# Six deep attention layers: exponential per 64-key piece with q's inverse norm as its scale, four new orders of work, and the feed-forward front moved by a third of a group

## The reference, cut to what matters

```python
qkv = x @ Wqkv
q = l2norm(q) * qs                      # per token and head
k = l2norm(k) * ksc
q = q * cos * scale + rotate_half(q) * sin * scale
k = k * cos / scale + rotate_half(k) * sin / scale
sim = einsum('bhwie,bhwje->bhwij', bq, bk2) * 8.0    # 32 queries against 64 keys
sim = where(mask, -max, sim)
attn = softmax(sim, -1)
out = einsum('bhwij,bhwje->bhwie', attn, bv2)
x = x + out @ Wo
xn = (x - mu) / sqrt(var + 1e-05) * g + bln
a, gate = split(xn @ W1 + b1)
x = x + a * gelu(gate) @ W2 + b2
```

## Time and profile before

| | us |
|---|---|
| median of 3 runs | 6133.31 (6131.36 to 6148.67) |
| the profiled execution, device time | 6136.03 |
| its span, first to last instruction | 6134.2 |
| first attention layer, 1399 to 2006 | 607 |
| first feed-forward block, 2006 to 2198 | 192 |

### The profile page before, as it was taken

The page is one execution under the profiler, slowest core; times in us unless marked ns, Lnnn a source line. Parts: engine busy times, 40 slices in busy tenths (PEclk is TensorE's granted clock), DMA queues, the critical chain, the costliest instruction groups (busy, mean ns, idle before and its releaser), DMA issues. The chain is left out here.

```text
span 6134.2 us, 175865 instructions
## 1 busy us (share of the span) xinstructions
PE 4713.8 (77%) x70592; PEld 3658.9 (60%) x70592; DVE 4298.2 (70%) x6496; ACT 2838.3 (46%) x5349; POOL 3353.0 (55%) x1834
## 2 busy tenths in 40 slices
PE   4986999947887678885788866888668887678875
PEld 3664877745666456664566655666546665466664
DVE  4346999958886478873688836888358884588854
ACT  2552333315554355552455534555335554355542
POOL 0004666637775367762577725777347774367741
PEclk8897999968998789986899978999778997798887
DMA  1000000002222012220122211222102222022220
GB/s 29 0 0 19 1 0 0 0 32 57 54 54 65 4 45 54 54 62 20 38 57 56 56 28 31 54 54 54 41 18 54 54 54 55 7 52 53 54 60 22
DMA packets 151608, 229.83 MB, mean 37 GB/s; under 512 B 33038, under 2 KB 56460, under 8 KB 149900
## 3 DMA queue, kind: packets, MB, share of 16 engines
q1 hardware_dynamic: 150924, 219.36, 15.0%
HBM read 26.31 MB, written 4.19 MB: 5 GB/s over the span
## 5 line engine op out<-in xcount | busy, mean ns | idle before, releaser
L1993 POOL TENSOR_TENSOR spare<-raw,table 128x512 f32<-128x512 f32 x768 | 1318.7, 1743 | 296.5 <-ACT spare L1592 296.5
L2003 POOL TENSOR_TENSOR raw<-raw,rs 128x1024 f32<-128x1024 f32 x384 | 821.8, 2151 | 694.5 <-DVE rs L1782 694.5
L1761 DVE TENSOR_TENSOR raw<-raw,spare 128x1024 f32<-128x1024 f32 x384 | 795.8, 2072 | 13.2
L1754 DVE TENSOR_TENSOR raw<-raw,table 128x1024 f32<-128x1024 f32 x384 | 736.8, 1919 | 62.3 <-POOL spare L1993 57.8
L1400 PE MATMUL trn<-ident,E 128*128 128x128 f32 x1536 | 329.5, 353 | 475.2 <-POOL E L2031 353.7
L1804 DVE TENSOR_REDUCE mx<-sco 128x16 f32<-128x1024 f32 x192 | 235.1, 1225 | 533.9 <-PE sco L1385 533.8
L2031 POOL TENSOR_TENSOR E<-E,rden 128x1024 f32<-128x1024 f32 x192 | 447.3, 2330 | 258.2 <-DVE rden L1819 258.2
L1400 PEld LDWEIGHTS trn<-ident,E 128*128 128x128 f32 x1536 | 237.3, 182 | 550.2 <-issue 366.2
L1611 ACT ACTIVATE room<-trn 128x512 f32<-128x512 f32 x384 | 230.1, 599 | 580.5 <-PE trn L1400 580.1
L1366 PE MATMUL trn<-ident,raw 128*128 128x128 f32 x3072 | 484.7, 281 | 9.2 <-ACT kT L1600 3.8
L1748 DVE TENSOR_REDUCE ss<-spare 128x16 f32<-128x1024 f32 x384 | 464.1, 1209 | 16.5 <-ACT spare L1592 16.4
(11 more groups left out here) (220 smaller groups left out, 11388.7 us busy)
## 6 DMA issues: line engine op xcount, KB each, us to landing
Vw<-V SPq DMA_DIRECT2D x1344, 128.0 KB
Vw<-V SPq DMA_DIRECT2D x192, 64.0 KB
spare<-in_L_ffn_Wqkv SPq DMA_DIRECT2D x6, 1536.0 KB, 6.6
wo<-in_L_ffn_Wo SPq DMA_DIRECT2D x6, 512.0 KB, 3.9
X<-in_L_attn_x SPq DMA_DIRECT2D x16, 128.0 KB, 2.6
x_before_deep<-X SPq DMA_DIRECT2D x1, 2048.0 KB, 8.3
raw<-x_before_deep SPq DMA_DIRECT2D x1, 2048.0 KB, 8.0
out<-X SPq DMA_DIRECT2D x16, 128.0 KB, 2.0
```

Of the source, the lines that this page charges most:

```text
L1754: dve.tensor_tensor(x, x, table[:, part, 0, k][:, None, :].to_broadcast([P, H, HD]), ALU.mult).then_inc(cos_part, 1)
L1761: dve.tensor_tensor(x, x, t2[:, part], ALU.add).then_inc(summed, 1)
L1993: pool.tensor_tensor(dst[:, :, a], src[:, :, 1 - a], table[:, part, 1, k, 32 * a:32 * a + 32][:, None, :].to_broadcast([P, H, 32]), ALU.mu ...
L2003: pool.tensor_tensor(x, x, rs[:, at:at + H][:, :, None].to_broadcast([P, H, HD]), ALU.mult).then_inc(rotated, 1)
```

## The change: what it does, and the diff

Three things.

1. q is no longer scaled by its inverse norm. PE turns it as soon as it is rotated, and the scores come out unscaled in q. DVE takes minus the maximum and multiplies its 16 values by the inverse norm (`nb`), which a copy `rq` keeps. ACT computes the exponential straight from `sco`, one 64-column piece at a time, with `rq` as scale and `nb` as bias: 16 instructions for each half. The difference on DVE is gone, POOL scales k alone, and `sco` is free when the exponentials are done (`exped`) instead of after the difference (`lowered`).
2. All tables of steps have new values. POOL normalises both halves in the next frame, PE turns them there, and v slot 9 is at step 3 (it was 5).
3. In `feed` the turn of group m+1 stands ahead of hidden tile 0 (it stood behind it), the return behind tile 0, statistics on DVE behind gate 0, normalising behind gate 1. `f_norm` and `f_affine` close the group's front.

```diff
-PROJ_STEPS = (-15, -14, -13, -12, -11, -9, -8, -7, -6, 5, 6, 13, 14)
+PROJ_STEPS = (-15, -14, -13, -12, -11, -9, -8, -7, -1, 3, 5, 8, 14)
...
-EXP_STEPS = (5, 13)
+EXP_STEPS = (4, 11)
...
-                sp.wait_ge(rotated, count(l * NSEQ * 4))
+                sp.wait_ge(summed, count(l * NSEQ * 4))
...
-                    pe.wait_ge(lowered, count(N))
+                    pe.wait_ge(exped, count(N))
...
-                act.wait_ge(lowered, count(N + 1))
-                e = E[:, o].rearrange("p s j -> p (s j)")
-                act.activation(e, e, ACT.Exp).then_inc(exped, 1)
+                if hp == 0:
+                    act.wait_ge(biased, count(N + 1))
+                for s in range(ROWS // 2):
+                    j, k = divmod(s, 2)
+                    h = 8 * o + 2 * j + hp
+                    c = hp * (ROWS // 2) + s
+                    t = act.activation(E[:, o, 2 * s + hp], sco[:, hp, s * HD:(s + 1) * HD], ACT.Exp,
+                                       bias=nb[:, o, c:c + 1], scale=rq[:, par, k, h:h + 1])
+                if hp == 1:
+                    t.then_inc(exped, 1)
...
+                dve.tensor_copy(rq[:, par], rs[:].rearrange("p (k a h) -> p k a h", k=2, a=2)[:, :, 0]).then_inc(q_scaled, 1)
...
-                dve.tensor_reduce(mx[:], s, AX.X, ALU.max).then_inc(maxed, 1)
+                dve.tensor_reduce(mx[:], s, AX.X, ALU.max, negate=True).then_inc(maxed, 1)
...
-                dve.tensor_tensor(E[:, o].rearrange("p (s h) j -> p h s j", h=2), s,
-                                  m[:, :, :, None].to_broadcast([P, 2, ROWS // 2, HD]),
-                                  ALU.subtract).then_inc(lowered, 1)
+                r = rq[:, par, :, 8 * o:8 * o + 8].rearrange("p k (j h) -> p h j k", h=2)
+                dve.tensor_tensor(nb[:, o].rearrange("p (h j k) -> p h j k", h=2, k=2),
+                                  mx[:].rearrange("p (h j k) -> p h j k", h=2, k=2), r,
+                                  ALU.mult).then_inc(biased, 1)
...
-                x = raw[:, par, k, part].rearrange("p (h d) -> p h d", d=HD)
-                at = (2 * k + part) * H
+                x = raw[:, par, k, 1].rearrange("p (h d) -> p h d", d=HD)
+                at = (2 * k + 1) * H
...
+                if front:
+                    f_in(m + 1)
                 for t in range(3):
                     f_hidden(m, t)
-                    if front:
-                        (f_in, f_return, f_norm)[t](m + 1)
+                    if front and t == 0:
+                        f_return(m + 1)
```

More of the change, by code:

```diff
@@ L1389, in scores, with turn_p @@
                     t.then_inc(scored, 1)
-            def turn_p(n, o, jj, tail):
+            def turn_p(n, o, jj, later, over):
                 N = 2 * n + o
+                step = FLIP_STEPS[o] + jj
                 if jj == 0:
@@ L1401, in turn_p, with mix @@
                 t.then_inc(p_turned, 1)
-            def mix(n, par, o, jj, first, tail):
+            def mix(n, par, o, jj, first):
                 N = 2 * n + o
@@ L1537, in feed @@
                             prepare(l + 1, step)
+                if front:
+                    f_norm(m + 1)
                 f_output(m)
```

141 lines of the change are left out of this document (79 added, 62 removed).

## The result

| | us | against before |
|---|---|---|
| before, median | 6133.8 | |
| after, median of 4 runs | 5977.6 (5956.3 to 5993.1) | 0.974 (95%: 0.970 to 0.978) |
| the profiled execution of after | 5956.3 (span 5954.4) | |

The change takes 156 us, 2.6%, give or take some 20. The forecast was 344 us, with 261 of them in the attention layers and 86 in the feed-forward blocks. The total lies just inside the wide range (5590 to 5990) and outside the 5690 to 5890 of the forecast itself; both parts were wrong, on opposite sides, so that the total lies in the range at all is partly luck.

What follows compares the result with a forecast made beforehand. It took a DVE and POOL wait cycle to bind now, V's moves with ACT's work afterwards. 6136 - 261 (attention) - 86 (feed-forward) = 5789, 5790 rounded; range 5690 to 5890, 8 in 10 5590 to 5990.

Steps and rivals of the forecast that it cites:

- The work of the engines: Busy time of a steady attention frame: DVE 31.8 to 30.1 us, POOL 27.4 to 23.1, ACT 21.6 to 29.1.
- The cycle of the moves: Attention frames: V's moves after slot 12, then ACT's work from slot 9 to slot 12, 13.6 + 20.5 = 34.1 us, would bind.
- the mean is 13.6: V's moves behind slot 12: from SP's first issue to the traffic's end, 14.4 and 12.8 us measured before.
- 4 to 7 us a frame: Sign that the forecast is right: ACT's first v piece idle this long before it, put down to a DMA.
- The 0.9 us for the clock: Added to each attention frame's 34.1 us because more PE waits may bring more of the lower clock, giving 35.0.
- the round trip over DVE and POOL: Old bound of the 37.56 us attention frame: scores wait for PE, PE for POOL, POOL for DVE's inverse norm; taken as gone.
- The layer's ends: Attention layer's ends, gains per layer: first frames 5 us, last frame but one 1.5, tail 4.
- I take 1.8 for all 48: Feed-forward front, placed a third of a group earlier: 1.8 us gained in each of 48 groups, 86 us in all.
- The moves' rival: Attention frames: moves end sooner or their wait falls into other waiting; frame 32.5 us, 195 us less, total 5595; chance 0.17.
- The clock's rival: PE falls to the lower clock after both waits; frame 37.0 us, feed-forward gain half, total 5988; chance 0.18.
- Slower: ACT's exponentials do not overlap, 0.46 us from start to start instead of 0.295; total 6201; chance 0.06.
- that the change does not do what it says: Rival for the whole change, given little room because each removed instruction is gone from the queues; no chance stated.

Runs made afterwards that it cites:

- moves in halves: The kernel after with V's 16 moves in two halves, eight after slot 10 and eight after slot 12, slots 9 and 11 each waiting for their own: 5809.5 us.
- V behind: The kernel after with V's first two pieces (slots 9 and 10) back at steps 5 and 6, behind the first half's exponentials: 5849.2 us.
- the one without the loop: The kernel after with PE's twelve steady frames of a layer written out instead of looped, the moves as they are: 5916.7 us.
- the front alone: The kernel before with only the feed-forward front placed a third of a group earlier, attention layers and step tables unchanged: 5971.7 us.
- halves and no loop: The kernel after with V's moves in two halves and PE's twelve steady frames of a layer written out: 5648.0 us, 0.921 of before.
- half the bytes: The kernel after with the same 16 moves a sequence, each of 256 columns instead of 512, which changes the result: 5935.2 us.

## Why the prediction was right and wrong

*The work of the engines.* Right for ACT in its sum: the exponentials are 0.289 apart (0.295 forecast), and ACT is busy for 28.5 to 28.8 us of a frame (29.1). That this came out so well is luck in part: an exponential is 0.467 long and not 0.394, and neighbours overlap by 0.18 and not by 0.10, and the two errors cancel. From slot 9 to slot 12 pass 20.6 us where slot 9 did not wait (20.5 forecast). DVE (25.4 to 26.6) and POOL (17.8) came out 4 to 5 us under the forecast of 30.1 and 23.1; the scaling on POOL alone went from 2.15 to 1.90 a piece. The trace does not say which neighbour had slowed them before. It made no difference, since neither was on the path. The Trainium skill's price for an exponential (ScalarE: Activation LUTs, What ACT_TABLE_LOAD costs), 332 ns from start to start, is 43 ns too much for this shape: neighbours overlap by 178 ns here and not by 93.

*The cycle of the moves.* Its mechanism was right. Two kernels that break the cycle in two places (moves in halves, V behind) show it, and so does the one without the loop, where it binds nearly every frame. The term that failed is "the mean is 13.6". It stood for SP's first issue to the end of the traffic, and for that, in the kernel before, it was right: the mean of 78 frames is 13.4. But the cycle runs from slot 12's drain to the piece that waits, which adds 0.8 ahead and 0.5 behind, and the stretch itself grew to 14.6 in the kernel after, with 220 long issues of SP where there were 138. Measured where slot 9 waits: 15.9 for the moves and 21.8 for ACT's work, 37.7 us, against 13.6 + 20.5 + 0.9 = 35.0. 2.3 of the 2.7 us are the moves'. Over all 72 steady frames the miss is 2.85 us, 205 of the 261 us that I forecast; the frames that do not wait for moves are as long for another reason (the loop's head, below). The sign "4 to 7 us a frame" of idle time ahead of the v piece did not come either: 43 waits of 2.6 us in 96 sequences. Of the stretch behind the last byte the Trainium skill speaks too (DMA: Bandwidth & Descriptors, Anatomy of one DMA — SWDGE (gpsimd) path): it puts most of the 2 us that a DMA costs beyond its bytes after the last byte, on the write's receipt. The page speaks of moves that GpSimd issues, and the trace does not agree for these, from SP and inside SBUF: from the last packet's end to the piece that waited pass 0.3 to 0.8 us.

*The 0.9 us for the clock.* Of fair size for what passes from PE to ACT, but the clock is not alone in it: where slot 9 waited, ACT's stretch is 1.3 us longer than the 20.5, since PE's pieces behind the wait come late.

*A wait that was not in the sum: the loop's head.* I asked what hides each edit, and did not ask what the removed wait had been hiding. The forecast said of the round trip over DVE and POOL only that it was gone. Inside its 5.2 us lay PE's 3.2 to 4.6 (3.8 in the mean) at a head. The heads cost 61 us beside the moves and 161 without them, 13 (most in the last layer) in the kernel before. The Trainium skill names the cause that fits (Runtime: NRT & Kernel Launch, Instruction fetch mechanics): instructions are prefetched in sequence, and a branch out of the window that is held must first fetch its target. The trace agrees: packets of instructions start with the waits, there are about two fewer for each jump that is gone, and the first pass of a layer, without a jump, has no wait.

*The layer's ends.* I gave the last frame but one 1.5 us less; it takes 34.5 on average against 31.9, with V pieces waiting 4.5 to 5.7 for the moves. The two intervals behind it went from 53.6 to 41.8 in layers 0 to 4, part of it by the later place of the addition. From a block's last addition to the next attention layer's last, 601.7 us became 603.6 on average in layers 1 to 5: attention took 1.9 us more a layer, where I had 43.5 less (the place of the addition and the rotation work that left the block are in these 1.9).

*The feed-forward front.* The 1.8 us a group was right for the groups that it was read from: the last layer's block went from 93.3 to 81.0 with the front alone, 1.76 in each of seven intervals, and PE's wait there is 2.2 us, inside the 1 to 2.5 forecast. The step that failed is "I take 1.8 for all 48". In a prepared block PE waited 31.5 us, 12.88 of them at once, these because the rotation stood between statistics and normalising in DVE's queue. In the kernel after, 24.3 of them are gone. PE's rows of one prepared block would have given 24 in each of five layers and 12 in the last, 132, where I had 86. The rest of the 163 lies mostly ahead of each block's first addition (171 to 151 us in sum), a stretch of which I had no term. The forecast did say that there was "a wait to take from", and did not read it.

*The rivals.* The moves' rival ("do not bind") was priced at 195 us by the forecast, and breaking the cycle gave 168. The clock's rival gave 5988 and lies nearest to 5978, with a frame of 37.0. Its mechanism is there in part: 15 frames at the lower clock behind a head's wait are 3.3 us longer than the other 15, 50 us in all. But it is not what the rival said: the mean granted clock of the whole run is 0.875 after and 0.866 before, PE's longest waits are at the heads, which it did not have, and the blocks gained twice their forecast instead of half. Slower, and that the change does not do what it says, are out.

*What came of it.* The kernel with the moves in halves and PE's loop written out takes 5648.0 us, 0.921 of before (0.919 to 0.923), with the exact work of the kernel after.

## What to carry to other kernels

Read a resource's cycle from the instruction that starts it to the one that waits for it, on the engine that waits; the time from the first issue to the last byte was 1.3 us less here, and it is no constant, since the change itself made it 1.2 longer. When a change removes a wait, ask what else stands still inside it, loop heads and fixed delays among them, since that is late next. And read each kind of group, not one for all: the last layer's groups stood for 8 of 48 and had waits of 3.5 us, and among the others was one of 12.9.

## What the runs showed of the hardware

- A jump back to PE's loop head costs 2.1 to 4.6 us of standing still, 2.9 in the mean after and 3.8 before, with a body of two frames of 638 products each. A body of four frames does not make it longer (12 waits, 2.8 in the mean). The first pass, without a jump, has no such wait. With each wait goes a packet of 16 KB in the queue that carries instructions.
- In straight code PE stands still without a releaser too, where it waits for little else: 0.9 us a frame in the kernel with halves and no loop (in the kernel before, written out, 0.9 in all), for up to 1.8 us at a time, mostly 613 to 615 products apart.
- SP issues the moves inside SBUF 0.64 us apart, but 220 of 1425 in the kernel after take over 0.9 (1.66 in the mean); at all 220 a packet of instructions was in flight, and at 44 of the 1205 short ones. The last packet of 16 moves ends 1.7 us behind the last issue, and 3.0 where an instruction packet lies between (52 of 54). From the producer to the waiting piece pass 15.9 us in the mean, 15.0 with half the bytes.
- Exponentials of 128x64 with scale and bias from SBUF are 467 ns long and 289 apart: an overlap of 178, where copies of 512 columns (about 600 long, 470 to 490 apart) overlap by 100 to 110.
